# A two-layer transformer kernel: normalisation, router products and expert scales rearranged ahead of the expert loop

## The reference

```python
x = x + _L0_xattn_ref(ctx, _layernorm(x), ...)
x = x + _L0_ffn_ref(_layernorm(x), ...)

def _L0_ffn_ref(tgt, Wr, br, W1, b1, W2, b2, gamma, beta):
    logits = jnp.einsum('bsd,ed->bse', tgt, Wr) + br
    top_v, top_i = jax.lax.top_k(logits, 2)
    top_w = jax.nn.softmax(top_v, axis=-1)
    ...
    h = jax.nn.relu(jnp.einsum('bsd,efd->bsef', tgt, W1) + b1)
    o = jnp.einsum('bsef,edf->bsed', h, W2) + b2
    return _layer_norm(tgt + sum over experts of router_w * o, gamma, beta)
```

## Time and profile before

| | us |
|---|---|
| median of 3 runs | 1811.26 |
| lowest and highest run | 1809.47, 1811.34 |
| time of the profiled execution | 1816.01 |
| its span | 1814.2 |
| mean granted clock of TensorE | 0.898 of full |

### The profile page before, as it was taken

How to read it: one execution, slowest core, us unless ns; L and a number is a source line. 1 busy time by engine, 2 the same in 40 slices (tenths; PEclk the granted TensorE clock), 3 DMA queues, 4 the chain that set the end, 5 groups by cost and what they waited for, 6 DMA issues and landing times.

```text
span 1814.2 us, 44910 instructions
## 1 busy us (share of the span) xinstructions
PE 1569.1 (86%) x18034; PEld 1287.9 (71%) x18034; DVE 1238.8 (68%) x2503; ACT 706.7 (39%) x1312; POOL 899.0 (50%) x862
## 2 busy tenths in 40 slices
PE   1889999999999999999999975399988856898798
PEld 0777788777777778777877763299977834565587
DVE  8757777777777577777777775244488566455765
ACT  1334444444433454444444431155544404232122
POOL 3246555655564356565556651477655506221322
PEclk9899999999999999999999996599999955555699
DMA  9124424443432243344343416477776480600101
GB/s 216 37 62 125 97 71 112 109 105 85 103 96 64 69 100 85 96 108 106 84 106 93 112 37 227 178 260 258 251 243 209 157 137 1 116 3 1 36 12 36
DMA packets 83376, 199.60 MB, mean 110 GB/s; under 512 B 17739, under 2 KB 40835, under 8 KB 82788
## 3 DMA queue, kind: packets, MB, share of 16 engines
q1 hardware_dynamic: 79428, 186.47, 38.5%
q0 software_dynamic: 3744, 10.26, 1.5%
HBM read 104.46 MB, written 39.72 MB: 79 GB/s over the span
## 4 chain that ended last, share of the span: by engine, by line
PE 51%; DVE 20%; POOL 7%; issue 6%; ACT 6%; DMA 5%; DVEq 1%; ACTq 0%; SPq 0%; POOLq 0%
PE ps L1921 20%; PE ps L2020 9%; PE ps L1954 5%; PE ps L2000 5%; PE ps L2001 5%; DMA latf<-wexp 4%; POOL PR L869 3%; DVE PR L1420 3%; ACT hf L1178 2%; POOL wst L881 2%; DVE hf L1606 2%; ACT hs_h L1180 2%; DVE mxs L1354 2%; PE ps L2285 2%; DVE wtmp L1448 1%
## 5 line engine op out<-in xcount | busy, mean ns | idle before, releaser
L869 POOL TENSOR_TENSOR PR<-PT 128x512 f16<-128x512 f32 (+1 forms) x416 | 441.3, 1071 | 423.8 <-ACT PT L1093 423.1
L1093 ACT ACTIVATE PT<-ps 128x512 f32<-128x512 f32 (+1 forms) x576 | 324.1, 597 | 367.3 <-PE ps L2001 367.0
L2020 PE MATMUL ps<-V_h,PT 128*128 128x65 f16 (+1 forms) x2304 | 325.2, 197 | 26.8 <-DVE PR L1420 21.1
L2020 PE MATMUL ps<-V_l,PT 128*128 128x65 f16 (+1 forms) x2304 | 320.5, 195 | 0.0
L2020 PE MATMUL ps<-V_l,PR 128*128 128x65 f16 (+1 forms) x2304 | 318.8, 194 | 0.0
L2020 PE MATMUL ps<-V_h,PR 128*128 128x65 f16 (+1 forms) x2304 | 318.3, 194 | 0.0
L2020 PEld LDWEIGHTS ps<-V_h,PT 128*128 128x128 bf16 (+1 forms) x2304 | 227.0, 99 | 121.9 <-issue 48.2
L1354 DVE TENSOR_REDUCE mxs<-ps 128x1 f32<-128x736 f32 x256 | 235.3, 919 | 48.3 <-PE ps L1954 48.2
L2000 PE MATMUL ps<-QA,KA 128*128 128x512 f32 (+1 forms) x576 | 248.5, 431 | 5.5 <-DMA QB<-maxT 4.9
L2001 PE MATMUL ps<-QB,KB 65*128 65x512 f32 (+1 forms) x576 | 231.8, 402 | 0.0
L2020 PEld LDWEIGHTS ps<-V_l,PT 128*128 128x128 bf16 (+1 forms) x2304 | 228.9, 99 | 0.6
(11 more groups left out here) (351 smaller groups left out, 3670.3 us busy)
## 6 DMA issues: line engine op xcount, KB each, us to landing
wup<-wsplit SPq DMA_DIRECT2D x46, 1024.0 KB
QA<-Q_h SPq DMA_DIRECT2D x64, 256.0 KB, 4.6
latf<-wexp SPq DMA_DIRECT2D x32, 512.0 KB, 4.4
wsplit<-wst SPq DMA_DIRECT2D x32, 512.0 KB, 2.9
KA<-K_h SPq DMA_DIRECT2D x32, 275.5 KB, 3.1
KA<-K_l SPq DMA_DIRECT2D x32, 275.5 KB, 4.0
KB<-K_h SPq DMA_DIRECT2D x32, 275.5 KB, 5.4
QB<-Q_l SPq DMA_DIRECT2D x32, 256.0 KB, 5.5
```

The source lines that it names most:

```text
L869: nc.gpsimd.tensor_tensor(PR[0:m, s % RING, :], PT[0:m, s % RING, :], upper(s)[0:m], ALU.subtract).then_inc(s_rem_pool, 1)
L1093: nc.scalar.activation(PT[0:m, s % RING, :], score_banks[s % 2][0:m], ACT.Exp, scale=HD ** -0.5).then_inc(s_exp, 1)
L2020: mm = nc.tensor.matmul(pv_bank[:, q, :], p, v, start=(kt == 0 and q == 0 and k == 0), stop=(kt == KT - 1 and k == 3), skip_group_check=True)
```

## The change

- `rstds` takes a number of columns, and groups 2 and 3 are normalised jointly: one `ln_sums` over eight token tiles, one power of eight columns, eight Y instructions that signal after four and after eight.
- In this stage (z = 0) group g has its own two PSUM banks, 2g and 2g + 1; its transposes no longer wait for `s_tfree`.
- PE puts the router products of group g - 2 ahead of the transposes of group g (g = 2, 3), and those of groups 2 and 3 behind. The product of group g goes into bank g. ACT copies the logits of group 0 ahead of the last `group_hi`, and the others behind it.
- DVE: statistics first, then the wait for the three loads and the split of the router weights, then `group_lo(0, 0)`, the eight Y instructions, `group_lo` of groups 1 to 3, the whole block of scales, and then the wait for the logits.
- `wscale`, `xscale`, `hscale` and `b1h` move to another region of SBUF, since their former place is XT's.

```diff
-        def rstds(pool, t0=None):
+        def rstds(pool, t0=None, n=4):
             powers[0] += 1
-            cols = slice(0, B) if t0 is None else slice(t0, t0 + 4)
+            cols = slice(0, B) if t0 is None else slice(t0, t0 + n)
...
-            return [ps[:, 0, :], ps[:, 1, :]] if z == 2 else [ps[:, 2, :], ps[:, 5, :]] if z == 3 else tbank
+            return [ps[:, 2 * g, :], ps[:, 2 * g + 1, :]] if z == 0 else [ps[:, 0, :], ps[:, 1, :]] if z == 2 else [ps[:, 2, :], ps[:, 5, :]] if z == 3 else tbank
...
-            for g in range(GR // 2, GR):
-                rstds(pool, 4 * g)
+            rstds(pool, TB, TB)
...
-            for g in range(GR):
+            def copy_group(g):
+                act.wait_ge(s_rt, g + 1)
+                nc.scalar.copy(LT0[:, g, :], ps[0:E0, g, :]).then_inc(s_lt, 1)
+
+            for g in range(GR - 1):
                 group_hi(0, g)
-            copy_logits(0, LT0)
+            copy_group(0)
+            group_hi(0, GR - 1)
+            for g in range(1, GR):
+                copy_group(g)
...
-            for g in range(GR // 2):
-                group_lo(0, g)
-                normalise(dve, X, Y, 4 * (g + GR // 2), 4, s_xn)
-            for g in range(GR // 2, GR):
-                group_lo(0, g)
+            ln_sums(dve, X, TB, TB)
             dve.wait_ge(s_in1, 16 * 3)
             nc.vector.tensor_copy(wrs["h"][:], wr_raw[:]).then_inc(s_wr, 1)
             dve.wait_ge(s_wr, 1)
             nc.vector.tensor_tensor(wrs["l"][:], wr_raw[:], wrs["h"][:].bitcast(F32), ALU.subtract).then_inc(s_wr, 1)
+            group_lo(0, 0)
+            lns[0] += 1
+            dve.wait_ge(s_rstd, lns[0])
+            for t in range(TB, NT):
+                ins = nc.vector.tensor_scalar(Y[:, t, :], X[:, t, :], ln_tmp[:, 0, t:t + 1], ln_tmp[:, 4, t:t + 1],
+                                              ALU.subtract, ALU.mult)
+                if t % 4 == 3:
+                    ins.then_inc(s_xn, 1)
+            for g in range(1, GR):
+                group_lo(0, g)
+            dve.wait_ge(s_b1, 32)
...
+            nc.vector.tensor_scalar(hscale[:], hscale[:], wscale[:, 14:15], 1.0 / 16384.0, ALU.mult, ALU.mult).then_inc(s_scales, 1)
             dve.wait_ge(s_route, 1)
...
-                    if k >= 2:
+                    if k >= 2 and z > 0:
                         pe.wait_ge(s_tfree, XJ * z + k - 1)
...
+            def route_group(g):
+                pe.wait_ge(s_tfree, 2 * g + 2)
+                pe.wait_ge(s_wr, 2)
+                product(ps[0:E0, g, :], [(wrs[v][:, 0, c, :], group(u, c, g)) for c in range(NC) for u, v in RANDL]) \
+                    .then_inc(s_rt, 1)
...
-            for g in range(GR):
-                transposes(0, g)
-            route(0, 0, LT0)
+            transposes(0, 0)
+            transposes(0, 1)
+            for g in range(2, GR):
+                route_group(g - 2)
+                transposes(0, g)
+            for g in range(2, GR):
+                route_group(g)
+            logits_to_rows(LT0, GR)
```

More of the change, by code:

```diff
@@ L174, in program @@
         sbx("unused1", [P, 8])
[L175 to L178, removed]
         oo = sbx("oo", [P, 3, D])
@@ L201, in program @@
         b1r = sb1("b1r", [P, E0, FC])
+        wscale = sb1("wscale", [P, 16])
+        xscale = sb1("xscale", [P, E0, NC])
+        hscale = sb1("hscale", [P, E0, 2])
+        b1h = sb1("b1h", [P, E0, FC])
         b2s = sb1("b2s", [P, E0, D])
@@ new lines, in _ @@
+            for g in range(1, GR):
+                group_lo(0, g)
+            dve.wait_ge(s_b1, 32)
+            rows = rowmax[:].rearrange("p (e s) -> p e s", s=PIECES)
+            nc.vector.tensor_reduce(wscale[:, 0:1], rows[:, :, 0:NC], AX.XY, ALU.max)
+            nc.vector.tensor_reduce(wscale[:, 1:2], rows[:, :, NC:], AX.XY, ALU.max)
+            nc.vector.tensor_reduce(wscale[:, 2:3], flat(b1r), AX.X, ALU.max, apply_absolute_value=True)
+            nc.vector.memset(wscale[:, 3:4], 0.0).then_inc(s_wb, 1)
@@ new lines, in _ @@
+            dve.wait_ge(s_wbr, 1)
+            link(dve, nc.vector.scalar_tensor_tensor(out=wscale[:, 8:9], in0=wscale[:, 4:5], scalar=2.0 * D, in1=wscale[:, 6:7],
+                                                     op0=ALU.mult, op1=ALU.add))
+            link(dve, nc.vector.tensor_scalar(wscale[:, 9:10].bitcast(U32), wscale[:, 8:9].bitcast(U32), 0x7F800000, None,
+                                              ALU.bitwise_and))
+            link(dve, nc.vector.tensor_tensor(wscale[:, 10:11], wscale[:, 9:10], wscale[:, 5:6], ALU.mult))
@@ new lines, in _ @@
+            nc.vector.reciprocal(wscale[:, 11:12], wscale[:, 10:11])
+            link(dve, nc.vector.reciprocal(wscale[:, 12:13], wscale[:, 4:5]))
+            nc.vector.tensor_scalar(wscale[:, 13:14], wscale[:, 10:11], 1.0 / 16384.0, 1.0 / 16384.0, ALU.mult, ALU.mult)
+            nc.vector.tensor_scalar(wscale[:, 14:15], wscale[:, 4:5], 1.0 / XSCALE, None, ALU.mult)
+            link(dve, nc.vector.tensor_scalar(xscale[:], rows[:, :, 0:NC], wscale[:, 12:13], XSCALE, ALU.mult, ALU.mult))
+            link(dve, nc.vector.tensor_scalar(hscale[:], rows[:, :, NC:], wscale[:, 11:12], 16384.0, ALU.mult, ALU.mult))
@@ L1516, in _ @@
+            for a in range(2):
+                ins = nc.vector.tensor_tensor(b1h[:, :, 4 * a:4 * a + 4], b1r[:, :, 4 * a:4 * a + 4],
+                                              hscale[:, :, a:a + 1].to_broadcast([P, E0, 4]), ALU.mult)
+            link(dve, ins)
+            nc.vector.tensor_scalar(hscale[:], hscale[:], wscale[:, 14:15], 1.0 / 16384.0, ALU.mult, ALU.mult).then_inc(s_scales, 1)
             dve.wait_ge(s_route, 1)
@@ L1563, in _ @@
             link(dve, nc.vector.tensor_tensor(rw[:, 3, :], rw[:, 1, :], rw[:, 2, :], ALU.mult))
[L1566 to L1582, removed]
-            link(dve, nc.vector.tensor_scalar(hscale[:], rows[:, :, NC:], wscale[:, 11:12], 16384.0, ALU.mult, ALU.mult))
-            for a in range(2):
-                ins = nc.vector.tensor_tensor(b1h[:, :, 4 * a:4 * a + 4], b1r[:, :, 4 * a:4 * a + 4],
-                                              hscale[:, :, a:a + 1].to_broadcast([P, E0, 4]), ALU.mult)
-            link(dve, ins)
-            nc.vector.tensor_scalar(hscale[:], hscale[:], wscale[:, 14:15], 1.0 / 16384.0, ALU.mult, ALU.mult).then_inc(s_scales, 1)
             experts = {}
@@ L2130, in route, with logits_to_rows @@
                                                  for c in range(NC) for u, v in RANDL]).then_inc(s_rt, 1)
-                pe.wait_ge(s_lt, GR * layer + GR)
+                logits_to_rows(LT, GR * layer + GR)
+            def logits_to_rows(LT, n):
+                pe.wait_ge(s_lt, n)
                 for t in range(NT):
```

## The result

The changed kernel takes 1802.39 us (median of 6 runs, 1798.19 to 1805.42) against 1811.3 for the kernel before (6 runs beside it, 1809.47 to 1813.44): ratio 0.9949, 95% interval 0.9931 to 0.9966. Measured again later (8 runs, 1795.62 to 1807.0) it took 1804.1 against 1809.48: 0.9966 (0.9952 to 0.9980). So the change gives about 5 to 9 us; 9.7 was forecast.

The account below looks back on a forecast made before the run. The prediction took a chain of waits, not work, to bound the passage from attention to the scatters. Logits 8.3 us earlier plus 1.4 from logits to scatter made 9.7 us: 1811.26 to 1801.6, range 1799.0 to 1807.3.

Parts of the forecast that it names:

- Start of the split: DVE's split of the router weights starts near 1105.7, behind a new wait for gamma and beta costing 2.1 us.
- Power of 8 columns: GpSimd's joint power takes 1.6 us, bounds 1.0 and 2.0, covered by the load wait.
- Products of group 0 and 1: PE's router products: group 0 from 1107.5 to 1110.0, group 1 from 1112.0 after the transposes of group 2.
- Clock rise: TensorE goes from low to high clock at 1112 to 1113.4, inside group 1's router products.
- Rival 1: TensorE's clock stays low through the router products: gain only 5.6 us, 1805.7; chance 0.2.
- Logits: Logits reach DVE at 1119.4 to 1120.1, 8.3 us earlier than before.
- Cover under the scales: DVE's block of scales runs from 1116.3 to 1119.5, hidden ahead of the logits by only 0.3 us.
- From logits to scatter: First scatter 10.85 us after the logits instead of 12.27, no longer behind the all-reduce: gain of 1.4 us.
- cheap first scatter: GpSimd's first scatter takes 0.35 us less than 1.31 if its extra was a fetch, now done while waiting.
- Rival 4: The scatters' start was bound by something other than the all-reduce: only 8.3 us left, 1803.0; chance 0.05.
- Rival 2: Gamma and beta land later, or another cover such as the scales' fails: around 1808.5; chance 0.1.
- Rival 3: GpSimd's all-reduce is held up until the `wdn` loads are through, delaying logits: 5.8 us slower, 1817.1; chance 0.05.

Follow-up runs that it names:

- Experiment 6: Changed kernel where the split of the router weights waits only for their own load, the other two being waited for at the scales: 1798.39 us, ratio to before 0.9942.
- experiment 2: Changed kernel with all router products behind all transposes and ACT's logit copies behind its last high part: logits at +20.21, span 1801.2 us.
- experiment 7: Filler transposes keep PE busy: 40 more in the changed kernel, logits +17.50, span 1789.9 us; 100 more in the kernel before, logits +26.04, span 1813.4.
- experiment 1: Kernel before with only the block of scales moved: 1807.92 us, ratio 0.9991; changed kernel with the scales put back behind the softmax: 1802.09 us, ratio 0.9967.
- experiment 9: Changed kernel with split load wait, early maxima, 26 filler transposes, reordered products, scatters waiting for slots alone: 1794.06 us, ratio 0.9916; the changed kernel was also repeated.
- experiments 8: Changed kernel with the router weights' own wait, b1 loaded second and the maxima right behind the sums: all-reduce at +12.36, logits +16.93, span 1796.8 us.
- Experiment 5: Changed kernel with groups 2 and 3 normalised separately again, two powers of four columns: logits at +22.75, span 1799.2 us.
- experiment 4: Changed kernel with the two shared transpose banks and all router products behind all transposes: logits at +23.44, span 1806.7 us.

## Why the prediction was right

Its steps one by one, as "+" times.

- **Start of the split**: forecast +5.9, measured +6.06, behind a DMA wait of 2.27 (2.1 forecast). Experiment 6 shows the wait to be on the path.
- **Power of 8 columns**: 1.6 by the slope of the earlier trace rows, measured 1.64, hidden under the load wait.
- **Products of group 0 and 1**: from +7.75 forecast, +7.72 measured; group 1's from +12.25 forecast, +11.80 measured. The 0.45 are not group 0's products (2.53 us against 2.5) but the eight transposes of group 2 between them: I had taken their 1.94 whole, yet the next product starts 1.55 after the first of them (1105.58 to 1107.13).
- **Clock rise**: forecast +12.3 to +13.6, measured +13.2 (1108.55), inside group 1's products. Rival 1 (clock low throughout, logits at +24.1) fell by this. Its reason, that transposes alone never raise the clock, fell with experiments 2 and 7: they do as soon as they run without gaps.
- **Last low part**: +16.25 to +16.85 forecast, +16.47 measured. **Logits**: +19.65 to +20.35, measured +19.95: 8.34 us earlier against 8.3.
- **Cover under the scales**: 0.3 us forecast, 0.58 measured, and thin indeed: in experiment 7 it is gone.
- **From logits to scatter**: 10.85 forecast, 10.68 measured, a gain of 1.59 against 1.4. I had put 0.10 and 0.38 between the end of `etu` and the first scatter; it took 0.32 (1125.64 to 1125.96). The cheap first scatter, which set part of the lower end of the range, did not come: it still took 1.31 us, long after the all-reduce.
- **Behind the scatters** nothing moved: 26.19 from the first scatter to the first up matmul (26.43 before), the loop +0.20. The move of the scales' tiles costs nothing that shows.
- **Rival 4** (scatters bound by something else) fell by experiment 1. **Rival 2** did not happen, though the landing of gamma and beta is the step with the largest scatter: 1.5 us in one of the eight traces that have this wait.
- **Rival 3**, the slower one, did not come either, but not for the reason I gave. Its "against" was a small transfer of the instruction queue amid full traffic. That says nothing of this delay: in the 8.44 us of experiment 9 and the 9.59 us of experiment 7 that queue moved no packet. What the runs show is that the delay ends long before the `wdn` loads are through, but is longer here than in rows 9: 6.84, 7.64, 8.06, 8.44 and 9.59 us (experiments 8, 1, 5, 9, 7), against 5.54 to 6.09 for the early all-reduce of rows 9 in all 14 traces. Between power and all-reduce the changed kernel has 11.38 us, a margin of 1.8 to 4.5, where I had worked out 5.7. Experiment 5 is what happens when it is used up.

Sum: 10.17 us in the passage against 9.7. The forecast for the time, 1801.6, is 0.8 from the median measured. The mechanism was forecast step by step and found so; the agreement of the time is partly luck. Measured again, the kernel before and the changed one were 5.4 us apart and not 8.9, both less than the 10.17 of the passage, and the profiled execution alone would have told 17.8. The opening of the prediction also left out a stretch: 18 of 64 us busy on TensorE skips 1123.3 to 1130.4, where it was busy for 4.0; the reading stands.

**What stays open.** The other 7.6 us of the profiled difference (4.42 ahead of the passage, 3.41 behind it, -0.2 in the loop) lie in code that was not changed: over all 14 traces attention ended between 1091.5 and 1100.1 and the rest took 368.0 to 377.4, and the repeat of the changed kernel differs from its first trace by 0.52 and 3.66 in these two. That they are chance is not shown. The three traces with the old order of the router's half end attention at 1099.3 to 1100.1, ten of the eleven others at 1098.5 or before; the medians show no gain of that size. The stretches at the low clock differ between the traces as well; why they do was not tested. Nor was what GpSimd's delay is, and what sets its length.

## What to carry to other kernels

Cut both traces at points around the edit before you compare: here 7.6 of the 17.8 us lay in code that was not touched, and the passage repeated to 0.1 us. Parts of a reordering can be substitutes, each seemingly worthless when undone alone (0.26 and 0.54 us) and worth 3.5 together, so undo them jointly too. When a wait is moved to an earlier place, list all that it counts: this one asked for 256 KB that its place did not need, and splitting it gave another 3.1 us up to the logits, 2.55 in the passage.

## What the runs showed of the hardware

An all-reduce on GpSimd behind elementwise work started late, by a delay in which the profile shows nothing: 5.54 to 6.09 us early in the span (14 traces, DMA share 0.38 to 0.49 from 58 to 64 us), 6.84 to 9.59 in the five kernels in which it shows in the passage, with DMA full. That traffic is the cause is not shown: among those five the longest delay had the lowest DMA share (9.59 us at 0.99) and the shortest a higher one (6.84 at 1.01), and the work ahead of the all-reduce is another than in the early one. Where the maxima came later than the delay ended, as in the changed kernel, it cost nothing. The Trainium skill (GPSIMD Engine Reference, section 2.1, Instruction dispatch) gives about 6 us for the first call of a freshly loaded kernel. The early delays agree with that figure, the later ones are up to 3.6 us longer; whether either is such a load no run here can show.

Transposes raise TensorE's clock. In experiment 7 PE ran nothing but fp32 transposes between 1103 and 1118, and the granted clock went from 0.50 (1.2 GHz) through 0.72 to 1.00 (2.4 GHz) there; in experiment 2 it rose 0.5 us behind 16 of them. The Trainium skill (TensorE: Matmul & The Clock Gate, Part 4: PE-mode transpose) says that they don't count as PE-busy in the same way and that the full clock doesn't engage for them; these traces disagree, as far as the kernel's transposes are of that mode: it calls them transposes, and the trace lists them as matmuls against the identity. Short pieces with gaps, such as three of 1.94 us in 8.3 us in experiment 4, left the clock low.

GpSimd's power on fp32 took 0.72, 1.01 and 1.64 us for 2, 4 and 8 columns: nearly linear, so one call of 8 saves only 0.4 of two calls of 4.
